# Relative-position heads: the read backs of the skewed rows move from SyncE to ScalarE, into a queue of their own

## The reference

```python
r = (r_emb @ Wr).reshape(2 * L - 1, NUM_HEADS, DEPTH).transpose(1, 0, 2)
AC = jnp.einsum('bhld,bhmd->bhlm', q + u_bias[None, :, None, :], k)
BD = jnp.einsum('bhld,hrd->bhlr', q + v_bias[None, :, None, :], r)
score = (AC + _rel_shift(BD)) / jnp.sqrt(jnp.float32(DEPTH))
attn = jax.nn.softmax(score, axis=-1)
out = jnp.einsum('bhlm,bhmd->bhld', attn, v)
```

## Time and profile before

| | |
|---|---|
| time, median of 3 runs | 1701.04 us (1699.28 to 1701.4) |
| the profiled execution's own time | 1699.04 us |
| its span, first to last instruction | 1697.2 us |
| mean granted TensorE clock | 0.948 of 2.4 GHz |
| PE / DVE / ACT busy, share of the span | 87% / 73% / 66% |
| all transfers | one queue for data, q1, 270.63 MB |

### The profile page before, as it was taken

How to read it: one execution, slowest core, us unless ns; L and a number is a source line. 1 busy time by engine, 2 the same in 40 slices (tenths; PEclk the granted TensorE clock), 3 DMA queues, 4 the chain that set the end, 5 groups by cost and what they waited for, 6 DMA issues and landing times. The chain is left out here.

```text
span 1697.2 us, 36694 instructions
## 1 busy us (share of the span) xinstructions
PE 1473.9 (87%) x12580; PEld 938.1 (55%) x12580; DVE 1234.0 (73%) x3703; ACT 1119.9 (66%) x2657; POOL 440.1 (26%) x442
## 2 busy tenths in 40 slices
PE   4688998989989885588888888769999999999996
PEld 2255555556555553366666666646555555555564
DVE  4367777777777765688888788663877878878755
ACT  1267676776767761567777677627888787887742
POOL 0333333333333313454544444330000000000001
PEclk9599999999999997899999999877999999999998
DMA  1677777788777745111001110007999999999920
GB/s 41 163 185 194 188 186 197 185 194 190 186 186 189 194 108 187 22 30 31 19 20 31 25 27 19 12 13 219 324 315 315 309 314 300 313 314 302 292 73 25
DMA packets 154904, 272.97 MB, mean 161 GB/s; under 512 B 27920, under 2 KB 31200, under 8 KB 154592
## 3 DMA queue, kind: packets, MB, share of 16 engines
q1 hardware_dynamic: 154720, 270.63, 56.3%
HBM read 148.03 MB, written 112.98 MB: 154 GB/s over the span
## 5 line engine op out<-in xcount | busy, mean ns | idle before, releaser
L519 ACT ACTIVATE a_Pm<-a_Pm,a_nm 128x272 f32<-128x272 f32 (+3 forms) x512 | 266.7, 570 | 167.3 <-DVE a_nm L441 166.7
L441 DVE CUSTOM_DVE_ANT_0 a_Pm<-ps,a_mask 128x272 f32<-128x272 f32 (+3 forms) x512 | 237.7, 503 | 92.3 <-PE ps L358 90.8
L1768 ACT COPY r_BD<-ps 128x320 f32<-128x320 f32 x512 | 200.4, 428 | 92.1 <-PE ps L1621 46.7
L1895 DVE CUSTOM_DVE_ANT_0 r_Sx<-ps,r_Sx 128x512 f32<-128x512 f32 x256 | 176.8, 691 | 108.8 <-PE ps L1634 107.2
L1621 PE MATMUL ps<-r_R,r_qv 32*128 32x320 f32 x1024 | 234.2, 498 | 3.2 <-ACT r_BD L1768 2.3
L358 PE MATMUL ps<-a_Kst,a_Qst 128*128 128x272 f32 (+4 forms) x640 | 200.6, 409 | 15.4 <-DMA a_Kst<-bounce 15.1
L1634 PE MATMUL ps<-r_K,r_qu 32*128 32x256 f32 x1024 | 199.7, 436 | 3.4 <-DVE r_nb L1895 3.4
L358 PEld LDWEIGHTS ps<-a_Kst,a_Qst 128*128 128x128 f32 x640 | 113.4, 193 | 146.3 <-issue 62.6
L1775 ACT ACTIVATE r_Sx<-r_Sx,r_nb 128x512 f32<-128x512 f32 x256 | 187.6, 733 | 7.9 <-DVE r_nb L1895 7.9
L1904 DVE COPY r_PT<-ps 128x512 f32<-128x512 f32 x256 | 175.9, 687 | 4.6 <-PE ps L1644 4.0
L373 PE MATMUL ps<-m_ident,a_Pm 128*128 128x128 f32 x1280 | 170.5, 278 | 1.6 <-ACT a_Pm L519 0.7
(11 more groups left out here) (204 smaller groups left out, 2745.9 us busy)
## 6 DMA issues: line engine op xcount, KB each, us to landing
spill<-r_BD SPq DMA_DIRECT2D x256, 288.0 KB, 5.0
r_Sx<-spill SPq DMA_DIRECT2D x128, 512.0 KB, 5.7
a_Kst<-bounce SPq DMA_DIRECT2D x128, 264.0 KB, 4.9
a_Qst<-bounce SPq DMA_DIRECT2D x128, 256.0 KB, 4.6
bounce<-a_kh SPq DMA_DIRECT2D x32, 264.0 KB, 3.5
bounce<-a_kl SPq DMA_DIRECT2D x32, 264.0 KB, 4.1
bounce<-a_qh SPq DMA_DIRECT2D x32, 256.0 KB, 5.7
bounce<-a_ql SPq DMA_DIRECT2D x32, 256.0 KB, 6.0
```

Source lines behind the costliest of these rows:

```text
L441: nc.vector.tensor_tensor_reduce(out=Pm[:, u % 2, qt, 0:w], in0=S[:, S_of[qt]:S_of[qt] + w], in1=mask[:, N + AV - w:N + AV], scale=-SCALE, ...
L519: nc.scalar.activation(row, row, ACT.Exp, scale=-1.0, bias=nm[:, u % 2, qt:qt + 1]).then_inc(exp_done, 1)
L1768: nc.scalar.copy(BD[:, m % BUFS, j, HW * half:HW * half + HW], ps[:, BDB[k % 3], 0:HW]).then_inc(bd_ev, 1)
L1895: nc.vector.tensor_tensor_reduce(out=row, in0=ps[:, AC + n % 2, :], in1=row, scale=-SCALE, scalar=-BIG, op0=ALU.add, op1=ALU.min, accum_ou ...
```

## The change

SP's loop now issues only the spills. The read back of pair `m - 2` is issued by ACT, at the end of its loop's body for pair `m`, behind that body's copies and exponentials. Its waits move with it: ACT now waits for the landing of spill `m - 2` and for PE's turn of pair `m - 8`. The transfer itself (source, target, size, semaphore) is the same; it goes into ACT's queue of transfers, where the spills are in SP's. Nothing changes on PE, DVE and POOL.

```diff
-            for k in range(PAIRS + 1):
-                if k < PAIRS:
-                    sp.wait_ge(bd_ev, 4 * (k + 1))
-                    if k >= SCRATCH:
-                        sp.wait_ge(rd[k % SCRATCH], 16 * (k // SCRATCH))
-                    ... (the two spills, as below)
-                if k >= 1:
-                    m = k - 1
-                    sp.wait_ge(wr[m % BUFS], 32 * (m // BUFS + 1))
-                    if m >= SCRATCH:
-                        sp.wait_ge(t_ready, 2 * (m - SCRATCH + 1))
-                    a = spill[m % SCRATCH]
-                    skew = bass.AP(tensor=a.tensor, offset=P - 1, ap=[[BW - 1, P], [P * BW, 2], [1, N]])
-                    sp.dma_start(Sx[:, m % SCRATCH], skew).then_inc(rd[m % SCRATCH], 16)
+            for k in range(PAIRS):
+                sp.wait_ge(bd_ev, 4 * (k + 1))
+                if k >= SCRATCH:
+                    sp.wait_ge(rd[k % SCRATCH], 16 * (k // SCRATCH))
+                rows_of = spill[k % SCRATCH].rearrange("t p n -> p t n")
+                sp.dma_start(rows_of[0:HP2, :, HP2:BW], BD[0:HP2, k % BUFS, :, HP2:BW]).then_inc(wr[k % BUFS], 16)
+                sp.dma_start(rows_of[HP2:P, :, 0:BW - HP2], BD[HP2:P, k % BUFS, :, 0:BW - HP2]).then_inc(wr[k % BUFS], 16)
...
+            def read_back(m):
+                act.wait_ge(wr[m % BUFS], 32 * (m // BUFS + 1))
+                if m >= SCRATCH:
+                    act.wait_ge(t_ready, 2 * (m - SCRATCH + 1))
+                a = spill[m % SCRATCH]
+                skew = bass.AP(tensor=a.tensor, offset=P - 1, ap=[[BW - 1, P], [P * BW, 2], [1, N]])
+                act.dma_start(Sx[:, m % SCRATCH], skew).then_inc(rd[m % SCRATCH], 16)
...
                             relative(n, part)
                     if has(2 * m + half - ELAG):
                         exps(2 * m + half - ELAG)
+                if 0 <= m - 2 < PAIRS:
+                    read_back(m - 2)
```

More of the change, by code:

```diff
@@ L1539, in _ @@
             sp.dma_start(wd.bitcast(I32), d["g_wd"]).then_inc(wd_in, 16)
-            for k in range(PAIRS + 1):
-                if k < PAIRS:
-                    sp.wait_ge(bd_ev, 4 * (k + 1))
-                    if k >= SCRATCH:
-                        sp.wait_ge(rd[k % SCRATCH], 16 * (k // SCRATCH))
-                    rows_of = spill[k % SCRATCH].rearrange("t p n -> p t n")
-                    sp.dma_start(rows_of[0:HP2, :, HP2:BW], BD[0:HP2, k % BUFS, :, HP2:BW]).then_inc(wr[k % BUFS], 16)
-                    sp.dma_start(rows_of[HP2:P, :, 0:BW - HP2], BD[HP2:P, k % BUFS, :, 0:BW - HP2]).then_inc(wr[k % BUFS], 16)
-                if k >= 1:
-                    m = k - 1
-                    sp.wait_ge(wr[m % BUFS], 32 * (m // BUFS + 1))
-                    if m >= SCRATCH:
-                        sp.wait_ge(t_ready, 2 * (m - SCRATCH + 1))
-                    a = spill[m % SCRATCH]
-                    skew = bass.AP(tensor=a.tensor, offset=P - 1, ap=[[BW - 1, P], [P * BW, 2], [1, N]])
-                    sp.dma_start(Sx[:, m % SCRATCH], skew).then_inc(rd[m % SCRATCH], 16)
+            for k in range(PAIRS):
[5 more added lines that the diff above has]
+                sp.dma_start(rows_of[HP2:P, :, 0:BW - HP2], BD[HP2:P, k % BUFS, :, 0:BW - HP2]).then_inc(wr[k % BUFS], 16)
             for k in range(SCRATCH):
```

## The result

The changed kernel takes 1715.26 us in the median of 5 runs (1714.4 to 1721.07), the kernel before, timed beside it, 1701.4 (1699.28 to 1706.52). The ratio is 1.0087, with an interval of 1.0063 to 1.011: slower. The forecast of 1708 named the side, and undersized it: 6.5 us were forecast and 14 came.

What follows compares the result with a forecast made beforehand. A spill's landing, its read back's issue and the next spill bound the stage at 3.56 us a pair, with PE and DMA nearly full. +5.8 for 115 pairs and +0.5 to 1 at the end made +6.5: 1708 us, range 1680 to 1735.

Steps and rivals of the forecast that it cites:

- Where the wait goes, and what stands behind it: ACT's read back of m - 2 waits ahead of pair m's last copy, which spill m needs; the loop moves to ACT.
- One sign that the prediction gave for being wrong: On ACT: waiting for PE instead of for spills, with DVE's and PE's waits shorter, would speak against the forecast.
- The issue on ACT, 0.37 us and hidden as work: ACT's read back issue, taken as 0.46 us with its gap: work 3.14 us a pair, covered below PE's 3.36.
- The rival of a dear issue: Issue on ACT takes 1.12 us, so ACT needs 3.80 a pair: +28 us and more, 1729 to 1740; chance 0.12.
- The length of the loop, where it binds: Spill to spill through ACT: two pairs take landing time 6.27 plus 0.95 us, so 3.61 a pair instead of 3.56.
- 115 x (3.61 - 3.56) = +5.8 us: The main term: 115 pairs outside the batch ends each grow from 3.56 to 3.61 us through the loop on ACT.
- it has no slack: before, ACT could run ahead of SP: Before, only spill m - 3 had to be down at pair m's first copy; the new loop lacks this; unpriced.
- the first case: The loop moves to ACT and gets a little longer: 1708 us, own range 1702 to 1729; chance 0.40.
- The stretches at 3.36 a pair: Stretches of the stage set by PE, as from 1346 us, would stop being set by PE and join the loop.
- two queues share the engines, so the kernel is faster: Engines alternate between queues, so spills land sooner: 1690 us at 3.46 a pair, 1678 if PE sets all; chance 0.35.
- The page's rule: ACT's and SP's transfers share 16 engines; a second issuer saves only issuing time, 0.46 us, here not even saved.
- Its floor is PE's 3.36: Of the 3.56 us a pair the change can move, PE's 3.36 is the floor; 115 x 0.20 = -23 us.

Runs made afterwards that it cites:

- e6_both: Kernel before, plus ACT's wait for spill m - 2 and a small transfer issued behind it; read backs stay on SP in one queue: 1705.89 us, ratio 1.006.
- e1_place: Changed kernel with ACT's read back of pair m - 3 issued behind the first copy of pair m: 1692.70 us, ratio 0.9982 to the kernel before.
- e7_one_copy: Changed kernel with the read back of pair m - 3 between the last copy of pair m - 1 and the first of m: 1696.3 us, ratio 1.0013.
- e9_lag3: Changed kernel with ACT issuing the read back of pair m - 3, not m - 2, at the same place: 1683.28 us, ratio 0.9932 to the kernel before.
- e4_issue: Kernel before, plus 128 small transfers issued by ACT at the end of each body, with no wait: 1701.22 us, ratio 1.0016.
- e5_again: The changed kernel run again without any edit, with a second profile: 1712.64 us, ratio 1.0103 to the kernel before.
- e8_pool: Changed kernel with the read backs issued by GpSimd in its own queue, each once its spill has landed: 1711.84 us, ratio 1.0092 to the kernel before.
- e3_sp2: Kernel before with SP issuing the read back of pair k - 2, not k - 1, behind spill k, in one queue: 1692.20 us, ratio 0.997.
- e10_sp2_later: One-queue kernel with SP's read backs two pairs behind, and everything behind the read back one step later (LAG 11): 1906.89 us, ratio 1.1237.
- e12_lag12: One-queue kernel with SP's read backs two pairs behind, and all behind them two steps later (LAG 12): four runs, 1900.14 to 2021.75 us, no ratio.

## Why the prediction was right, and what it undersized

- **Where the wait goes, and what stands behind it: right.** ACT waits ahead of the read back for the landing, the copy and the spill follow 0.41 and 0.86 us behind the issue, and SP waits for copies alone. e6_both makes that loop without a second queue of read backs and costs 0.6%. e1_place, e7_one_copy and e9_lag3 keep the queue and take the wait from ahead of the last copy, and are 0.9% to 1.7% under the changed kernel. One sign that the prediction gave for being wrong came in part: ACT waits for PE longer than for spills at its copies (57.7 us against 32.4). PE's and DVE's waits did not get shorter, though, so it is no sign of a faster loop here.
- **The issue on ACT, 0.37 us and hidden as work: right** (366 ns median, 670 at most; e4_issue, +0.16%, not told from nothing). The rival of a dear issue falls.
- **The length of the loop, where it binds: close, and its match in us is luck.** Parted at 4.6 us, the ordinary intervals give +5.7 and +5.0 (e5_again) beside the +5.8 of the forecast, but that line was drawn afterwards, and at 5.0 us they give +14.7. The loop holds in about half of the pairs (59 of 126), not in all. Its two parts were each a little off: 0.86 for 0.95 us behind the landing, and a spill that in the median waits 6.19 us for its read back, where it was 6.51 before and 6.27 was forecast.
- **The term that was mis-sized is 115 x (3.61 - 3.56) = +5.8 us.** The mean pair went from 3.57 to 3.72 us, +17.8 us in the stage (+0.10 a pair and +11.3 in e5_again), and the batch ends, at nothing in the forecast, added 5.5 (4.5). The forecast priced a loop in which each landing takes the mean time. It wrote "it has no slack: before, ACT could run ahead of SP" and gave that no price. Its price is the larger part: 12 more intervals over 4.6 us. Of the 23.4 us some 7.5 (the estimate above) came through the clock, which the forecast left at its upper level. That long landings stop ACT and that the clock falls behind three of them is seen in the rows; that this time is all the clock's and the slack's was not separated by a run. Whether the second queue has a share in the long intervals stays open: e8_pool has 20 of them without the wait, e1_place and e9_lag3 have 9 and 8 with two queues, and e6_both's 8 are from an unusually fast execution.
- **The time itself.** 1715.26 lies in the range of the first case, 1702 to 1729, at twice the forecast's step. What lies around the stage was 7.1 us shorter in the profiled execution, for which the forecast had no reason; without that it would have been further off.
- **The stretches at 3.36 a pair: not shown.** Only 12 of the 127 intervals before lie within 0.03 us of 3.36, and 15 now, so the stretch of the earlier trace rows was rare already, and there was little to lose. The median interval went from 3.54 to 3.58 us. In e1_place 51 lie there and in e9_lag3 69.
- **The rival "two queues share the engines, so the kernel is faster"** is not borne out. Spills of the changed kernel land in 4.8 us instead of 5.0, but so they do in one queue when the read back has the same lead (4.7 in e6_both), and in e1_place, with two queues, they take 5.3. No cost of the second queue shows on ACT either (e1_place and e9_lag3 are no slower than before); for GpSimd that is open.
- **The page's rule.** By the Trainium skill, "DMA: Bandwidth & Descriptors", section "Issuing engines are not separate DMA queues", a second issuer saves only the issuing time. The change agrees with it in that nothing was won, and so do the landings of the table, which don't depend on the number of queues. e9_lag3 won 0.7%, more than the 0.3% of e3_sp2, which takes the loop away with one issuer. No run shows whether that difference is the issuing time, which in e3_sp2 is 1.06 us a read back on SP by the median, or something else.
- **The reading of before was right on the loop and too simple on its worth.** "Its floor is PE's 3.36" promised 23 us for a kernel without the loop. e3_sp2 and e1_place have no such loop and won 0.3% and 0.2% (the latter not told from nothing). Only e9_lag3 came to half of it, 446.6 us of stage against 458.4. Its count of four batch ends for 12 intervals is off by one, as only three lie inside; with three, the other pairs still take 3.57.

## What to carry to other kernels

Price a moved wait by what stands behind it at its new place, and by how often it is met when it is reached: here waiting for a spill one pair older, on the same line, turned +0.9% into -0.7%, with the read back now issued behind the next spill and not ahead of it. A mean interval prices a loop and not its lost slack; count the late arrivals in the trace (here 21 landings of over 7 us) and ask which engine each of them will stop. A wait and an issue that each cost little alone (+0.25%, +0.16%) came to +0.6% in a row; the intervals are too wide to say that this is more than their sum. Before profiles of two kernels are compared, see whether each execution is near its kernel's median.

## What the runs showed of the hardware

- The clock fell right behind three waits of ACT of 2.3 to 2.7 us (PE was busy 1.68 of 3.00 us from 1187 to 1190, 1.78 from 1430 to 1433 and 2.04 from 1495 to 1498), in a stage where PE was else busy nearly all the time, and in the kernel before behind one of 2.45 us. Another wait of ACT, 2.20 us for PE at 1349, was not followed by a fall: the window from 1346 to 1360 has PE busy 13.18 of 14 us at 1.00. And the clock stayed at 1.2 GHz for 275 us in e10_sp2_later and e12_lag12 with PE busy in 275.00 of 275 us by the profile, and rose later in the same stage, at the same work. What held it down the runs do not tell.
- Matmuls of 32 rows in different blocks of rows ran beside each other (1.68 us a step), in the same block they did not (2.12).
- Read backs issued on SP right behind a spill (e3_sp2) took 1.06 us to issue by the median, against 0.37 on ACT for the same transfer.
- A spill's landing went with the lead of the read back ahead of it, 5.3 us at 0.1 us and 4.6 to 4.8 at 1.0 to 1.1 us, and 4.4 to 4.5 with the read back issued behind it, in one queue and in two.
